# A two-layer transformer kernel with hand-written engine orders: another order of its start and its end, and the token permutation moved from VectorE to GpSimd and ScalarE

## The chip, the cores and the metric

One core of a Trainium2 chip, one launch. The metric is the device time of that core in microseconds (us). Five engines run their own instruction streams and wait for each other by semaphores: TensorE (matmuls and transposes), VectorE, ScalarE (activations and copies), GpSimd, and SyncE, whose queue here issues nearly all DMAs.

## The reference

The input `x` is 2 x 1024 tokens of 256 channels; everything is f32 unless said.

```
x  = L0_attn_x                                   # (2, 1024, 256)
xn = layernorm(x)
x  = x + L0_attn(xn) + L0_ffn(xn)
xn = layernorm(x)
x  = x + L1_attn(xn) + L1_ffn(xn)

L0_attn: q = rope(xn@Wq+bq) 32 heads of 8; k, v 8 heads of 8 (each serves 4 q heads)
         causal softmax(q k^T / sqrt 8) v over the 1024 tokens, @ Wo + bo
L0_ffn:  e4m3 inputs, bf16 results: (gelu(xn@Wg0) * (xn@Wg1)) @ Wl, hidden 1024
L1_attn: q, k, v 16 heads of 16, rope on q and k; the softmax runs over the 16 heads
         of one token: scores "bshd,bstd->bsht", then "bsht,bstd->bshd", @ wo^T
L1_ffn:  weights quantised to -s, 0, +s per group of 64; silu(gate)*up,
         RMS norm, @ w_proj^T, hidden 1024
```

Biases and some weights are scaled by constants before the call, which changes no shape.

## The kernel before, in words

The 2048 tokens are 16 tiles of 128, eight to a batch. Every step of every tile is a small Python function named by what it makes (`xnT.3` is step `xnT` of tile 3), and a table `ORDER` writes out for each engine in which order it runs its steps. Every step first waits on counting semaphores for its inputs and for its output buffer; an engine runs its steps strictly in the listed order, so a step that waits holds up all that are listed behind it. The same is true of SyncE's DMA issues. A second pass with exact number ranges stands behind a branch, and is not taken for these inputs; the steps `rng`, `rngb`, `fl` and `flagT` at the end decide that.

*Layer 0, attention.* For a tile: `ln0` (VectorE) and `rs0` (GpSimd) give mean and inverse deviation, `xn` the normalised tile, `xnT` its transpose (TensorE), `xnTc` the copy to SBUF, `qkv` the projection, `qkvc` the copy with bias, `va` the values, `wide` a range check. `rope` (four GpSimd instructions) turns q and k; `qh` (ScalarE) and `ql` (GpSimd) write the high and low half of q as f16, `q0` and `kl` (VectorE) those of k. `qt` and `kt` (SyncE) are DMA transposes of the two. Then come the *quads* Q: for tile n one for each earlier tile of its batch, itself, and each half of the heads: tile 0 has Q0 and Q1, tile 1 Q2 to Q5, tile 2 Q6 to Q11. `qk.Q` makes four score blocks of 128 x 512, `exp.Q` is two exponentials of 1024 columns, `mask.Q` (GpSimd, on the diagonal) zeroes the future, `pv.Q` is eight matmuls into the bank `psV`; `ob`, `obT`, `att`, `attT`, `attTc`, `wo0`, `xa` finish the tile.

*Layer 0, feed forward.* `up` (four a tile), on ScalarE `g`, `sq`, `fh`, `th` and on VectorE `ge1`, `ge3` for the gelu of each half, `down`, `yff`. The weights come by `wg` (SyncE) and `wgx` (ScalarE's queue) and are rounded to f8 by `w8.0` to `w8.5`. 

*Layer 1, attention.* `ln1`, `rs1`, `xn1`, `xs` (two f16 halves), `xt` (DMA transpose), `qkv1` (two a tile). The even part of `qkv1` holds q and k, the components on partitions and the 128 tokens in columns. `rab` (VectorE) multiplies it from PSUM by a cosine and a sine table, two instructions of 512 columns; `rr` (GpSimd) makes the difference and the sum, two of 256 columns; `rw` writes both to DRAM (`rscr`), `rd` reads them back so that four groups of 32 tokens lie in four partition quadrants (into `qk1T`), and `kq` (ScalarE, two copies of 512) puts them in the order in which `S1` (16 small f32 matmuls) wants them: for each of four j, 128 columns of 16 heads x 8 tokens. The tokens of one such group are 16 apart, since `vw` and `vr` bring the values in that order. So between PSUM and `S1` the tokens have to be permuted once; before, `rab` writes them transposed (token a*16+c to column c*8+a) and `kq` reads runs of eight. `ex1` (the exponentials), `PV1`, `o1r`, `o1T`, `o1`, `osum` (a range check), `ow` and `at1r` (through DRAM), `at1T`, `at1Tc`, `wo1`, `yo`.

*Layer 1, feed forward.* The three-valued weights are made once from `wt` loads by `tc`, `ts`, `tsc`, `tm`, `tcs`, `td`, `tde`, `tr`, `tw`. Then `gu` (four a tile), `tg`, `sg`, `hh`, `ssq`, `ssm`, `rsg`, `hxa`, `hx`, `ht` (DMA transpose), `dn1` (16 matmuls), `yout`, `out`.

*Loads and tables.* `first.0` x of tile 0, `first.1` Wqkv, `first.2` x of tiles 1 to 3; `lx` (ScalarE's queue) the rest of x; `lc` five small loads with Wo; `lw` the layer 1 attention weights (waits for `w8.3`), which `wh` and `wl` split; `wg.4` and `wg.5` wait for `w8.0` and `w8.1`, `wt.2` for `tc.0`. `tab` (VectorE, nine operations) reduces the angles of layer 1, `sin` (ScalarE) makes four tables of them and needs another activation table than the exponential. `tT`, `tTc` turn them.

*Warm products.* `warm.n` is `WARM[n]` matmuls of a block of ones into `psV` that nobody reads; before there are seven, 39 matmuls, all ahead of the first `pv`. The eight PSUM banks are four `psS`, `psV`, and `psA`, `psB`, `psC` that all other steps share in the order of `ORDER["pe"]`, each waiting for the reader of the bank's last content.

The order of TensorE's last steps before is, word for word:

```
        "qkv1.30 PV1.13 gu.57 qkv1.31 S1.14 o1T.13 gu.58 at1T.12 dn1.12 wo1.12 PV1.14 gu.59 gu.60 o1T.14 at1T.13 dn1.13 "
        "wo1.13 S1.15 gu.61 gu.62 PV1.15 gu.63 o1T.15 at1T.14 wo1.14 dn1.14 at1T.15 wo1.15 dn1.15 flagT.0"),
```

## Time and profile before

| what | value |
|---|---|
| median of 3 runs | 557.74 us (557.38 to 558.65) |
| the profiled execution | 560.62 us, its span 558.9 us |
| busy in the span: TensorE, ScalarE, VectorE, GpSimd | 520.7, 471.9, 381.5, 233.8 us |
| mean granted TensorE clock | 0.979 of full |
| DMA | 46.18 MB in 211344 packets |

The span is from the first to the last instruction of the profiled execution; its own time also has what lies around the span. An engine's busy time tells how much of the span it works, not whether anything waits for it; where two engines are full at once, the stretches, the waits and the chain of work that ended last have to be read together. A line number names a line of the kernel; a line in a helper serves many steps (L674 and L675 are every pair of transposes).

### The profile page before, as it was taken

The numbers are of one execution on the slowest core, as the hardware profiler recorded it, in microseconds if no ns is written. First come the engines' busy times: TensorE is split into PE (matmuls) and PEld (weight loads), VectorE is DVE, ScalarE is ACT, GpSimd is POOL, SyncE is SP. The second block draws the span as 40 slices with busy tenths as digits, with TensorE's granted clock in tenths as the row PEclk, the third lists the DMA queues.
The fourth block names the chain that finished last, engine by engine and source line by source line (L and its number), as shares of the span: only waits on it lengthen the run. The fifth ranks groups of instructions, "written<-read, shape, count | busy, mean of one in ns | idle before, by whom it ended". The sixth has DMA issues, their size and how long they took to land.

```text
span 558.9 us, 12847 instructions
## 1 busy us (share of the span) xinstructions
PE 520.7 (93%) x4872; PEld 261.7 (47%) x4920; DVE 381.5 (68%) x794; ACT 471.9 (84%) x614; POOL 233.8 (42%) x299
## 2 busy tenths in 40 slices
PE   7678999999999999999999999999999999998875
PEld 3323335434354555545555455564455353556544
DVE  5838887788779767766676787656554544756755
ACT  0579999999999999999989989988898998974440
POOL 3556745726534246344664565133082220160200
PEclk8869999999999999999999999999999999999988
DMA  7932112112443622345306454564533318347863
GB/s 246 326 84 58 26 41 57 41 33 39 76 82 47 103 47 59 53 66 79 67 12 122 62 83 67 93 99 67 110 56 66 64 40 142 67 83 130 112 112 88
DMA packets 211344, 46.18 MB, mean 83 GB/s; under 512 B 198544, under 2 KB 207888, under 8 KB 211280
## 3 DMA queue, kind: packets, MB, share of 16 engines
q1 hardware_dynamic: 208832, 42.37, 41.0%
q10 hardware_dynamic: 2448, 2.95, 1.7%
q8 instruction: 40, 0.66, 0.5%
q14 instruction: 24, 0.20, 0.1%
HBM read 19.09 MB, written 10.49 MB: 53 GB/s over the span
## 4 chain that ended last, share of the span: by engine, by line
PE 68%; ACT 13%; DVE 7%; DMA 5%; issue 4%; SPq 1%; POOL 1%; ACTq 0%; DVEq 0%
PE psV L775 20%; PE psS L761 8%; ACT Pt L1057 6%; PE psC L961 3%; PE psS L914 3%; PE psA L961 2%; PE psC L971 2%; PE psB L961 2%; DMA at<-o2scr 2%; DVE r L1512 2%; DMA stage<-in_wg 2%; PE psC L853 2%; PE psB L971 2%; PE psB L812 1%; PE psA L853 1%
## 5 line engine op out<-in xcount | busy, mean ns | idle before, releaser
L1057 ACT ACTIVATE Pt<-psS 128x1024 f32<-128x1024 f32 x288 | 279.9, 1031 | 27.2 <-PE psS L761 22.6
L775 PE MATMUL psV<-Pt,vaug 128*32 128x512 f32 x1152 | 150.6, 606 | 1.3 <-POOL Pt L1753 0.9
L1753 POOL TENSOR_SCALAR_AFFINE_SELECT Pt<-Pt 128x1024 f32<-128x1024 f32 x64 | 71.9, 1148 | 70.9 <-ACT Pt L1057 70.9
L761 PE MATMUL psS<-qTf,kTf 32*128 32x512 f16 x576 | 69.0, 388 | 7.7 <-DMA kTf<-QXf 4.2
L761 PEld LDWEIGHTS psS<-qTf,kTf 32*128 32x128 f16 x576 | 18.6, 91 | 92.3 <-ACT Pt L1057 47.0
L1805 POOL TENSOR_TENSOR ss<-ss,mhalf 128x1 f32<-128x1 f32 x16 | 9.3, 582 | 92.5 <-DVE ss L1589 92.5
L775 PEld LDWEIGHTS psV<-Pt,vaug 128*32 128x32 f32 x1152 | 25.0, 108 | 39.9 <-issue 31.1
L1131 ACT ACTIVATE stage<-psS 128x1024 f32<-128x1024 f32 x32 | 31.0, 1021 | 8.9 <-PE psS L914 8.8
L1799 POOL TENSOR_TENSOR rqkv<-r 128x256 f32<-128x256 f32 x32 | 24.9, 800 | 30.0 <-DVE r L1512 30.0
L1733 POOL TENSOR_TENSOR rt<-qkv,cs 128x320 f32<-128x320 f32 x16 | 15.1, 942 | 44.5 <-DVE QXf L1334 35.1
L1744 POOL TENSOR_TENSOR QXf<-rt,QXf 128x512 f16<-128x512 f32 x16 | 21.2, 1327 | 28.9 <-ACT QXf L1044 28.9
L1427 DVE SCALAR_TENSOR_TENSOR ga<-gw,gb 128x512 bf16<-128x512 f32 x32 | 23.1, 722 | 6.1 <-ACT gw L1083 6.1
L1418 DVE SCALAR_TENSOR_TENSOR gw<-gw,gb 128x512 f32<-128x512 f32 x32 | 25.1, 783 | 2.3 <-ACT gw L1072 2.2
L961 PE MATMUL psC<-wguT,xhs 128*128 128x512 bf16 x90 | 23.7, 380 | 2.4 <-issue 1.7
L1595 DVE SCALAR_TENSOR_TENSOR qtmp<-qtmp,ss 128x1024 f16<-128x1024 f32 x16 | 22.5, 1408 | 3.2 <-ACT qtmp L1152 3.2
L1152 ACT ACTIVATE qtmp<-qtmp,ss 128x1024 f16<-128x1024 f32 x16 | 18.5, 1158 | 4.5 <-POOL ss L1805 4.4
L1736 POOL TENSOR_TENSOR rt<-qkv,sn 128x160 f32<-128x160 f32 x32 | 21.9, 706 | 0.0
L1072 ACT ACTIVATE gw<-gb 128x512 f32<-128x512 bf16 x32 | 20.9, 653 | 0.0
L1083 ACT ACTIVATE gw<-gw 128x512 f32<-128x512 f32 x32 | 20.7, 646 | 0.0
L1512 DVE TENSOR_TENSOR r<-psC,big 128x512 f32<-128x512 f32 x14 | 14.5, 1120 | 8.9 <-PE psC L853 8.9
L1147 ACT ACTIVATE qtmp<-qtmp 128x1024 bf16<-128x1024 f32 x16 | 17.0, 1060 | 3.9 <-DVE qtmp L1583 2.4
L914 PE MATMUL psS<-kTf 24*128 24x128 f32 x512 | 19.5, 283 | 0.0
(339 smaller groups left out, 1088.1 us busy)
## 6 DMA issues: line engine op xcount, KB each, us to landing
rscr<-rqkv SPq DMA_DIRECT2D x32, 128.0 KB, 2.8
qk1T<-rscr SPq DMA_DIRECT2D x64, 64.0 KB, 3.0
vscr<-rqkv SPq DMA_DIRECT2D x16, 128.0 KB, 3.3
o2scr<-o SPq DMA_DIRECT2D x16, 128.0 KB, 1.7
at<-o2scr SPq DMA_DIRECT2D x16, 128.0 KB, 3.3
out<-yout SPq DMA_DIRECT2D x16, 128.0 KB, 2.7
x<-in_x ACTq DMA_DIRECT2D x3, 512.0 KB, 5.5
stage<-in_wg SPq DMA_DIRECT2D x2, 512.0 KB, 9.8
```

The lines of the kernel that those rows point to most:

```text
L761: e.matmul(psS[j], kd[32 * j:32 * j + k, h, 128 * at:128 * at + 128], qd[32 * j:32 * j + k, 4 * h:4 * h + 4, :].rearrange("p s n -> p (s n ...
L775: ins = e.matmul(psV[32 * j:32 * j + 32, :], vaug[:, at, j, 32 * h:32 * h + 32], Pt[(4 * Q + j) % NP], start=(kb == 0 and h == 0), stop=(k ...
L914: ins = e.matmul(psS[b][:, 128 * j:128 * j + 128], of_group(n, 1, b, j), of_group(n, 0, b, j), start=True, stop=True)
L961: ins = e.matmul(bank[:], src[:, pt, 128 * c:128 * c + 128], wguT[:, c, c0:c0 + 512], start=(k == 0), stop=(k == 3))
L1057: e.activation(flat(Pt4[:, u % NP:u % NP + 2, :]), flat(psS4[:, j:j + 2, :]), ACT.Exp, scale=scale).then_inc(S["exp"], 1)
L1131: e.activation(P1[:, 4 * b:4 * b + 8, :].rearrange("p g n -> p (g n)"), flat(psS4[:, b:b + 2, :]), ACT.Exp, scale=SC1).then_inc(S["ex1"], 1)
L1418: e.scalar_tensor_tensor(gw[:, half, :], gw[:, half, :], 1.0 / GA, gb[:, half, :], ALU.add, ALU.mult).then_inc(S["ge1"], 1)
L1427: e.scalar_tensor_tensor(a, gw[:, half, :], 1.0, gg, ALU.add, ALU.mult).then_inc(S["ge3"], 1)
L1512: e.tensor_tensor(r1[:, k, :].rearrange("p (e s c a) -> p e s a c", e=2, s=2, a=8), bank, table.unsqueeze(2).to_broadcast([128, 2, 2, 8, 1 ...
L1595: e.scalar_tensor_tensor(hx_b[:, 1, :], h1, sn[:, 2:3], hx_b[:, 0, :], ALU.mult, ALU.subtract).then_inc(S["hx"], 1)
L1753: e.affine_select(out=p, in_=p, pattern=[[0, 8], [1, 128]], compare_op=ALU.is_ge, fill=0.0, base=0, channel_multiplier=-1).then_inc(S["mas ...
L1799: e.tensor_tensor(dst[:, 256 * f:256 * f + 256], r1[:, f, 0:256], r1[:, f, 256:512], op).then_inc(S["rr"], 1)
```

## The change

Five things change at once.

1. SyncE's and ScalarE's queues at the start: `lc`, then `wt.0`, `wg.0`, `wg.1`, then the transposes `qt.0 kt.0`, and only then the loads that wait (`wg.4`, `lw.0`, `wg.5`, `wt.1`, `wt.2`). On ScalarE `lx.1 lx.2` go first, `wgx` after `tc.0`, `sin.0` before `exp.0`, and `g`, `fh`, `sq` of the first halves and `wh.0` behind the first exponentials. On VectorE `qkvc.0`, `tab.0`, `q0.0 kl.0` go ahead of the weight roundings `w8`; on TensorE `up.0` to `up.3` go behind the first quads.
2. The permutation: `rab` writes its products in plain token order; `rr` reads runs of four tokens 16 apart and writes contiguously; the scratch `rscr` is laid out with the quadrant ahead of q and k; `kq` reads with a step of four floats (16 bytes) from SBUF; the constant `same` of the second pass follows.
3. `WARM` is now 24 matmuls in four places at the start and 14 in six places (`warm.4` to `warm.9`) among the last steps; those wait for the last `ob`, when `psV` is free.
4. The range check `rng.0` moves behind `at1Tc.15`; in the drain `rd.15` goes ahead of `out.11`, `dn1.13` ahead of `at1T.13`, `osum.14` behind other steps.
5. All five orders are written anew; most steps move by a few places.

The set of steps is the same but for the warm products. The diff, cut to its core:

```
 KQ = 2
-WARM = (9, 3, 2, 7, 5, 11, 2)
+COLD = 4
+WARM = (9, 3, 10, 2, 3, 2, 2, 3, 2, 2)
...
-        "warm.0 xnT.0 qkv.0 warm.1 xnT.1 warm.2 qkv.1 warm.3 up.0 up.1 up.2 ts.0 warm.4 ts.1 up.3 warm.5 qk.0 warm.6 "
...
+        "warm.0 xnT.0 qkv.0 warm.1 xnT.1 qkv.1 warm.2 xnT.2 ts.0 qkv.2 qk.0 warm.3 qk.1 ts.1 pv.0 qk.2 pv.1 up.0 qk.3 "
+        "up.1 xnT.3 up.2 obT.0 pv.2 qk.4 td.0 td.1 up.3 pv.3 qk.5 up.4 up.5 qkv.3 pv.4 qk.6 up.6 up.7 qk.7 pv.5 xnT.4 "
...
+        "S1.14 o1T.13 gu.58 at1T.12 dn1.12 wo1.12 PV1.14 gu.59 gu.60 warm.4 o1T.14 warm.5 dn1.13 at1T.13 warm.6 wo1.13 "
+        "S1.15 gu.61 gu.62 PV1.15 gu.63 o1T.15 at1T.14 dn1.14 wo1.14 warm.7 at1T.15 warm.8 wo1.15 warm.9 dn1.15 flagT.0"),
...
-        "wgx.2 wgx.3 qh.0 g.0 tc.0 g.1 sq.0 fh.0 fh.1 wh.0 qh.1 sq.1 lx.1 lx.2 exp.0 th.0 exp.1 sin.0 exp.2 exp.3 qh.2 "
+        "lx.1 lx.2 qh.0 tc.0 wgx.2 wgx.3 sin.0 qh.1 exp.0 exp.1 exp.2 lx.3 g.0 exp.3 fh.0 sq.0 g.1 qh.2 sq.1 th.0 wh.0 "
+        "tde.0 exp.4 tde.1 fh.1 exp.5 fh.2 th.1 g.2 exp.6 sq.2 fh.3 g.3 exp.7 th.2 exp.8 exp.9 g.4 qh.3 sq.3 exp.10 "
...
-        "vz.0 ln0.0 xn.0 idc.0 xnTc.0 ln0.1 ln0.2 xn.1 qkvc.0 w8.0 xnTc.1 va.0 w8.1 w8.2 wide.0 w8.3 q0.0 qkvc.1 ln0.3 "
+        "vz.0 ln0.0 xn.0 idc.0 xnTc.0 ln0.1 ln0.2 qkvc.0 xn.1 wide.0 va.0 xnTc.1 tab.0 q0.0 kl.0 qkvc.1 xn.2 xnTc.2 "
+        "wide.1 va.1 ln0.3 w8.0 w8.1 q0.1 kl.1 qkvc.2 ln0.4 tsc.0 wide.2 tsc.1 w8.2 w8.3 xn.3 ob.0 xnTc.3 tm.0 va.2 "
...
+        "hh.28 v1c.15 o1.13 at1Tc.12 sg.29 yo.12 yout.12 hh.29 osum.13 o1r.14 sg.30 ssm.14 o1.14 osum.14 at1Tc.13 hx.14 "
+        "yo.13 yout.13 hh.30 sg.31 o1r.15 hh.31 o1.15 at1Tc.14 ssm.15 osum.15 hx.15 yo.14 at1Tc.15 yout.14 rng.0 rngb.0 "
+        "yo.15 yout.15 fl.0"),
...
-        "first.0 first.1 first.2 wg.0 wg.1 wg.4 wt.0 lc.0 wt.1 lw.0 wg.5 wt.2 qt.0 kt.0 qt.1 kt.1 qt.2 kt.2 qt.3 wt.3 "
+        "first.0 first.1 first.2 lc.0 wt.0 wg.0 wg.1 qt.0 kt.0 wg.4 qt.1 kt.1 lw.0 wg.5 wt.1 wt.2 qt.2 kt.2 qt.3 wt.3 "
+        "kt.3 qt.4 wt.4 wt.5 qt.5 xt.0 kt.4 xt.1 rw.0 mk.0 kt.5 rw.1 rd.0 xt.2 vw.0 rd.1 vr.0 ht.0 qt.6 xt.3 vw.1 kt.6 "
...
-        "vw.13 rd.12 vr.12 ow.11 vw.14 vr.13 at1r.11 rd.13 rw.14 ht.12 xt.15 rd.14 ow.12 vr.14 at1r.12 rw.15 ow.13 "
-        "vw.15 ht.13 at1r.13 out.11 rd.15 out.12 vr.15 ow.14 ht.14 at1r.14 ow.15 at1r.15 out.13 ht.15 out.14 out.15"),
+        "ht.13 at1r.13 rd.15 out.11 out.12 ow.14 vr.15 ht.14 at1r.14 ow.15 out.13 at1r.15 ht.15 out.14 out.15"),
...
-        rscr = nc.dram_tensor("rscr", [NT, 2, 4, 16, 512], F32, kind="Internal").ap()
+        rscr = nc.dram_tensor("rscr", [NT, 4, 2, 16, 512], F32, kind="Internal").ap()
         vscr = nc.dram_tensor("vscr", [NT, 16, 128, 16], F32, kind="Internal").ap()
         o2scr = nc.dram_tensor("o2scr", [NT, 16, 128, 16], F32, kind="Internal").ap()
         oscr = nc.dram_tensor("oscr", [NT, 128, 256], F32, kind="Internal").ap()
...
             return (qk1Tg if n < NT else qk1T)[:, s, :, :]
 
         def landed(s):
-            return qk1T[:, s, :, :].rearrange("p j n -> p (j n)").rearrange("p (h j a) -> p j h a", j=4, a=8)
+            return qk1T[:, s, :, :].rearrange("p j n -> p (j n)").rearrange("p (m j) -> p j m", j=4)
+
+        def by_run(a):
+            return a.rearrange("p (m b j) -> p b m j", b=4, j=4)
 
         def of_group(n, s, b, j):
 
...
 
             def rw(n):
                 src = flat(rqkv[n % 2][:, 0:2, :]).rearrange("p (f m t) -> p f m t", f=2, t=32)
-                dst = rscr[n].rearrange("s b (f i) (h t) -> f (i h) (s b) t", f=2, t=32)
+                dst = rscr[n].rearrange("b s (f i) (h t) -> f (i h) (b s) t", f=2, t=32)
                 for f in range(2):
                     w.wait_ge("rr", 2 * n + f + 1)
                     e.dma_start(dst[f], src[:, f, :, :]).then_inc(S[f"d_rw{n % 2}"], 16)
...
                 w.wait_ge("kq", KQ * n)
                 for b in range(4):
                     dst = qk1T[32 * b:32 * b + 16, :, :, :].rearrange("p s j n -> p s (j n)")
-                    e.dma_start(dst, rscr[n, :, b].rearrange("s d n -> d s n")).then_inc(S[f"d_rd{n % 2}"], 16)
+                    e.dma_start(dst, rscr[n, b].rearrange("s d n -> d s n")).then_inc(S[f"d_rd{n % 2}"], 16)
 
             def ow(n):
                 w.wait_ge("o1", 2 * n + 2)
...
 
             def warm(n):
                 w.wait_ge("zero", 5)
+                w.wait_ge("ob", NT if n >= COLD else 0)
                 for _ in range(WARM[n]):
                     e.matmul(psV[:], blockb[:], blockb[:].unsqueeze(1).to_broadcast([128, 4, 128]), start=True, stop=True)
 
...
                 w.wait_ge(f"d_rd{n % 2}", read_groups(n))
                 w.wait_ge("S1", 4 * n)
                 for s in range(2):
-                    e.activation(qk1Tg[:, s, :, :].rearrange("p j (h a) -> p j h a", a=8), landed(s), ACT.Copy).then_inc(S["kq"], 1)
+                    e.activation(qk1Tg[:, s, :, :], landed(s), ACT.Copy).then_inc(S["kq"], 1)
 
             def ex1(n):
                 w.wait_ge("w8", 6)
...
                                 ALU.mult).then_inc(S["v1c"], 1)
 
             def rab(n):
-                bank = psM[filled["qkv1", 2 * n] % len(psM)][:].rearrange("p (e s a c) -> p e s a c", e=2, s=2, a=8)
+                bank = psM[filled["qkv1", 2 * n] % len(psM)][:].rearrange("p (e s t) -> p e s t", e=2, s=2)
                 t0 = 128 * (n % NB)
                 w.wait_ge("tTc", 5)
                 w.wait_ge("tc", 12)
                 w.wait_ge("qkv1", 2 * n + 1)
                 w.wait_ge("rr", 2 * n)
                 for k in range(2):
-                    table = turns[:, k:k + 2, t0:t0 + 128].rearrange("p e (a c) -> p e a c", a=8)
-                    e.tensor_tensor(r1[:, k, :].rearrange("p (e s c a) -> p e s a c", e=2, s=2, a=8), bank,
-                                    table.unsqueeze(2).to_broadcast([128, 2, 2, 8, 16]), ALU.mult).then_inc(S["rab"], 1)
+                    e.tensor_tensor(r1[:, k, :].rearrange("p (e s t) -> p e s t", e=2, s=2), bank,
+                                    turns[:, k:k + 2, t0:t0 + 128].unsqueeze(2).to_broadcast([128, 2, 2, 128]),
+                                    ALU.mult).then_inc(S["rab"], 1)
 
             def ro1(n):
                 cb = cos1[:, n % NB, :].unsqueeze(1).unsqueeze(1).to_broadcast([128, 2, 16, 8])
...
                 w.wait_ge("rab", 2 * n + 2)
                 w.wait_ge(f"d_rw{n % 2}", 32 * (n // 2))
                 for f, op in enumerate((ALU.subtract, ALU.add)):
-                    e.tensor_tensor(dst[:, 256 * f:256 * f + 256], r1[:, f, 0:256], r1[:, f, 256:512], op).then_inc(S["rr"], 1)
+                    e.tensor_tensor(dst[:, 256 * f:256 * f + 256].rearrange("p (b m j) -> p b m j", b=4, j=4),
+                                    by_run(r1[:, f, 0:256]), by_run(r1[:, f, 256:512]), op).then_inc(S["rr"], 1)
 
             def rsg(n):
                 sn = ss[n % len(ss)]
...
     s[:, :, 0::2] *= -1
     mneg = np.where(p[None, :] > p[:, None], np.float32(NEG), np.float32(0))
     pos = (np.arange(8)[None, :] * 128 + p[:, None]).astype(np.float32)
-    same = (np.arange(512)[None, :] % 8 == np.arange(8)[:, None]).astype(np.float32)
+    same = (np.arange(512)[None, :] // 4 % 8 == np.arange(8)[:, None]).astype(np.float32)
     ind2 = np.stack([NEG * same, 1.0 - same]).astype(np.float32)
     one = (p[:, None] // 16 == np.arange(8)[None, :]).astype(np.float32)
     ind1 = np.stack([NEG * one, 1.0 - one], axis=1).astype(np.float32)
```

## Rows read from the trace of the kernel before

**Rows 1.** Stretches: us, each engine's busy time (instructions), granted clock, DMA share, GB/s.

```profile
60.00:250.00 190.00, 182.71 (x1680) 88.62 (x1692) 147.34 (x302) 186.01 (x252) 89.99 (x111) 1.00 0.31 56
250.00:495.00 245.00, 242.08 (x2370) 120.78 (x2388) 154.53 (x324) 221.90 (x280) 101.27 (x128) 1.00 0.44 75
530.00:559.00 29.00, 18.15 (x148) 12.51 (x147) 14.96 (x41) 8.48 (x12) 1.10 (x2) 0.88 0.54 105
```

The busy times are those of PE, PEld, DVE, ACT and POOL, in that order.

**Rows 2.** The chain that ended last, before 60 us: start, duration, what.

```profile
21.35 2.01 SPq L608
23.46 6.31 DMA kTf<-QXf
```

**Rows 3.** ScalarE's instructions in order of time, 30 to 60 us: start, duration.

```profile
30.49 1.94 ACT L1057 ACTIVATE Pt<-psS 128x1024 f32<-128x1024 f32 x2 [3.93 <-PE psS L761]
...
34.79 1.28 ACT L1018 ACT_TABLE_LOAD   x1
...
39.13 1.28 ACT L1057 ACT_TABLE_LOAD   x1 [0.56 <-PE psV L775]
...
48.81 3.96 ACT L1057 ACTIVATE Pt<-psS 128x1024 f32<-128x1024 f32 x4
```

**Rows 4.** GpSimd's instructions in order of time, tile 0's rope and `ql`.

```profile
11.67 1.17 POOL L1733 TENSOR_TENSOR rt<-qkv,cs 128x320 f32<-128x320 f32 x1 [0.19 <-DVE qkv L1303]
...
15.96 1.15 POOL L1744 TENSOR_TENSOR QXf<-rt,QXf 128x512 f16<-128x512 f32 x1 [0.74 <-ACT QXf L1044]
```

**Rows 5.** Stretch 19 to 24 us, busy time of `tab` alone (VectorE, then ScalarE).

```profile
19.00:24.00 5.00, 3.92 (x9) 0.00 (x0) 0.70 1.05 394
```

**Rows 6.** Line 600, the key transposes: from issue to landing.

```profile
DMA to landing us min/median/max: 2.3/2.8/6.3
```

**Rows 7.** Groups of instructions by line: busy us, mean ns, idle before, releasers.

```profile
L1512 DVE TENSOR_TENSOR r<-psC,big 128x512 f32<-128x512 f32 x14 | 14.5, 1120 | 8.9 <-PE psC L853 8.9
L1583 DVE SCALAR_TENSOR_TENSOR qtmp<-stmp,psB 128x512 f32<-128x512 f32 x13 | 8.9, 686 | 5.6 <-PE psB L961 5.3
L1799 POOL TENSOR_TENSOR rqkv<-r 128x256 f32<-128x256 f32 x32 | 24.9, 800 | 30.0 <-DVE r L1512 30.0
L1744 POOL TENSOR_TENSOR QXf<-rt,QXf 128x512 f16<-128x512 f32 x16 | 21.2, 1327 | 28.9 <-ACT QXf L1044 28.9
L1122 ACT ACTIVATE kTf<-qk1T 128x512 f32<-128x512 f32 x32 | 18.6, 642 | 0.1
```

**Rows 8.** Line 1512, `rab`: who waited for it, us and times.

```profile
  PEld psA L858: 1.2, 1
```

**Rows 9.** TensorE's instructions in order of time, from 530 us.

```profile
533.07 0.33 PE L674 MATMUL psB<-identf,at 128*128 128x128 f32 x1 [2.96 <-DMA at<-o2scr]
...
533.35 2.98 PE L971 MATMUL psC<-wpT,stmp 128*128 128x256 bf16 x16
...
537.73 1.17 PE L914 MATMUL psS<-kTf 24*128 24x128 f32 x32
...
546.51 1.91 PE L971 MATMUL psC<-wpT,stmp 128*128 128x256 bf16 x16
...
553.34 2.48 PE L971 MATMUL psC<-wpT,stmp 128*128 128x256 bf16 x16
```

**Rows 10.** Other engines' instructions in order of time, from 530 us.

```profile
531.88 1.06 ACT L1147 ACTIVATE qtmp<-qtmp 128x1024 bf16<-128x1024 f32 x1 [1.57 <-DMA stmp<-qtmp]
...
535.12 1.15 ACT L1122 ACTIVATE kTf<-qk1T 128x512 f32<-128x512 f32 x2
...
548.50 1.32 SPq L624 DMA_TRANSPOSE stmp<-qtmp  x1
548.53 0.68 DVE L1625 TENSOR_REDUCE hl<-rec 128x1 f32<-128x512 f32 x1
...
551.00 0.41 DVE L1602 COPY at1T<-psA 128x256 f32<-128x256 f32 x1
```

**Rows 11.** DMA issues by line: count, and median us from issue to landing.

```profile
stmp<-qtmp SPq DMA_TRANSPOSE x16, 4.2
```

29 lines of the change are left out of this document (17 added, 12 removed), and 232 rows, old and new, of the table ORDER.

## The prediction

> **What bounds the kernel now.** I read the stretches first. From 60 to 250 us ScalarE is busy 186.01 of 190 us and TensorE 182.71; from 250 to 495 us TensorE is busy 242.08 of 245 us and ScalarE 221.90; from 530 us on nobody is full (TensorE 18.15 of 29 us) and the granted clock falls to 0.88 [rows 1]. So there are four stages: a start in which the softmax cannot begin, a stage set by ScalarE, one set by TensorE with ScalarE 10% free, and a drain of dependent steps. VectorE and GpSimd bound none of them; an edit of theirs counts only by whom it lets go earlier.
>
> The chain that ended last tells what holds the start: not arithmetic, but SyncE's queue reaching the first transposes at 21.35 and 23.46 us, and 6.31 us until the keys landed [rows 2]. ScalarE's order of time shows the first exponentials at 30.49 us, Q6's (the end of tile 1, start of tile 2) in the row that starts at 48.81 us, and two table loads of 1.28 us around `sin` in between [rows 3].
>
> **Part A, the start.** Tile 0's rope begins at 11.67 us, 0.19 us after GpSimd was free of the three `rs0`, which precede it in both orders; so it does not move. `ql.0` ends at 15.96 + 1.15 = 17.11 us [rows 4]. `qt.0` could go then, but SyncE still stood at `lw.0`, `wg.5` and `wt.2`, which wait for `w8` and `tc.0`. The new order puts `qt.0 kt.0` ahead of every bulk load that waits. `lc` comes first now because `tab.0` precedes `q0.0 kl.0` on VectorE; the nine `tab` operations take 3.92 us and some gaps, say 4.2 us [rows 5]. From the end of `xnTc.1`, some 1 us after tile 0's rope began, that gives `kl.0` at 17.6 us if `lc`'s five loads have landed, as bulk loads now stand behind and not before them. `qt.0` takes 2.01 us of queue as before, so `kt.0` is issued at 19.2 us instead of 23.46: 4.3 us earlier.
>
> The landing is unknown, as other loads share the 16 engines: `lx.1`, `lx.2` now go early, the two `wgx` loads (1 MB) at about 17.7 us. Bounds are the fastest key transpose, 2.3 us, and the 6.3 us of this one [rows 2, 6]; with less outstanding than before I take 4.3, the middle. Then keys are there at 23.5 us. Four score matmuls (0.6 us) and a table load follow: `sin.0` now runs before `exp.0`, which therefore has to load its table again, and a load stands behind the wait of its instruction, as the row at 39.13 us shows. So `exp.0` starts at 23.5 + 0.6 + 1.28 = 25.4 us, not 30.49.
> [...]
>
> From `exp.0` to the start of Q6 the kernel before took 20.2 us (half of the 3.96 us row is Q5, so Q6 is at 50.7 us). I listed ScalarE's steps before Q6 in both orders: they are the same set. So the shift there is what ScalarE idles less. `sin` with its loads (34.79 to 40.42 us, 5.6 us) leaves this stretch; `g` `fh` `sq` of halves 0 and 1 (six steps of some 0.5 us, start to start) and `wh.0` (1.5 us), 4.5 us in all, enter it, as `up.0` to `up.3` and `lw.0` now come later. A new hole stands between `exp.1` and `exp.2`: `qk.2` is behind `pv.0`, which waits for GpSimd's mask (two of 1.1 us), some 1.8 us. Q6 is at 25.4 + 20.2 - 5.6 + 4.5 + 1.8 = 46.3 us, 4.4 us earlier. The next tile's chain (`rope.2` after `mask.1` at 30.4 us, `qh.2`, `ql.2`, transposes) gives keys by 44 us, before they are needed. With the landing's bounds it is 2.4 to 6.4 us.
>
> Does it last? As long as ScalarE is the bound, yes, since the set of its steps is the same; but TensorE has only 7.3 us free from 60 to 250 us and 2.9 after [rows 1]. Its moved work (four `up` later, one `xnT` and `qkv` earlier) about cancels. I take 3.5 of 4.4 us; ends 0 (all lost to TensorE) and 6.
>
> **Part B, the permutation.** `rab` writes with a step of eight floats and takes 1.12 us; `hh`, also 512 f32 elements with one operand in PSUM, but contiguous, takes 0.69 us [rows 7]. Contiguous `rab` should be 0.69: 32 x 0.43 = 13.8 us less of VectorE, which is hidden except where somebody waits. TensorE waited for `rab` to free a bank a few times, 1.2 us at most [rows 8]. Four to five such waits can each shrink by up to 2 x 0.43 = 0.86 us, but some only pass to the next step. I take 1.2 us, ends 0 and 4.
>
> `rr` on GpSimd (800 ns, 256 elements) now reads runs of four floats. `ql`, 512 elements with a broadcast, takes 1327 ns [rows 7]: its price follows the count and not the pattern. I keep 0.80 us, at the dearest 1.33; GpSimd has idle time all along but for the drain, where two would cost 1 us. The DMA sides of `rw` and `rd` keep their pieces (128 bytes and 2 KB), so nothing is taken for them.
>
> `kq` is the doubtful one. It read runs of eight floats; now every element is 16 bytes from the last. It takes 642 ns for 512 elements [rows 7], no more than fits the exponential's 0.97 us for 1024 [rows 3], so its runs of eight cost nothing today and a gain is excluded; no row has ScalarE reading with a step. The lower bound is no change. The upper bound is what the step costs VectorE in `rab`, 0.43 us each. I take no change, since `rab`'s step is twice as wide and on the write side, and keep both ends.
> The Trainium skill (Advanced Engine Details and Errata, "SBUF Cachelines") says that two accesses should fall into one 16-byte line, and that a new line at each access is penalised. By that rule `kq` pays; `rab`'s row agrees for a step of 32 bytes, no row here tests 16. It speaks against this change and is the first rival below.
>
> **Part C, the drain.** Three things move. First, `rd.15` stood behind `out.11` in SyncE's queue and `dn1.13` behind `at1T.13`, for which TensorE idled 2.96 us until 533.07; then `dn1.13` ran slowly (2.98 us against 1.91 for the 16 matmuls of `dn1.14`) [rows 9], and `S1.15` came only at 537.73. Now `dn1.13` runs when its transpose has landed (`ssq.14` waited for the same until 531.88) [rows 10], in that hole, with warm products around it, and `wo1.13` ends at 535.6. `S1.15` then waits for `kq.15`, which ends at 535.12 + 1.15 = 536.3 [rows 10] behind `hxa.14` and does not move: 1.4 us gained. Second, `osum.14` leaves the place before `hh.31`: 0.3 us. Third, the range checks `rng` (from 548.53 us) stood before `at1Tc.15` (551.00) and now come after, so `wo1.15` starts about 1.5 us earlier. `dn1.15` then waits for its transpose `ht.15`, issued at 548.50 before [rows 10] and at 546.8 now; with the median of such a landing, 4.2 us [rows 11], it starts at 551.0 and takes 1.9 us, where it ran from 553.34 for 2.48 [rows 9]. The end of TensorE's work moves from 555.8 to 552.9: 2.9 us in all, of which 1.7 are the first two. `rng` and `rngb` still fit beside `dn1.15`. The 14 warm products cost at most 14 x 0.22 = 3 us where they delay; they stand in front of waits, so I take 0. Upstream, `rab.14` and `rab.15` are on the chain: 0.6 us more. Part C: 3.5 us, ends 1 (what the transposes' landings give is lost) and 5.
>
> **The sum.** 3.5 + 1.2 + 3.5 = 8.2 us. The profiled execution took 560.62 us, its span 558.9; it becomes 552.4. The median of the runs shown is 557.74, 2.9 below that execution: 549.5 us.
>
> **The rivals.**
> - ScalarE pays for `kq` (20%). 32 x 0.43 = 13.8 us. Eight of them before 250 us count fully, 3.4 us; sixteen between 250 and 495 us, 6.9 us against 23.1 us of ScalarE's idle time, one third, 2.3; in the drain two on the way to `S1.15`, 0.9. Together 6.6: 556.1 us. For it: `rab`'s price for a step. Against it: half the step, another engine.
> - The slower side (10%): the same price, but none is hidden, because `kq` stands ahead of exponentials for which TensorE waits: 549.5 + 13.8 = 563.3. It decides from 8.2 / 32 = 0.26 us per `kq` on. For it: ScalarE 98% busy until 250 us [rows 1]. Against it: its 10% free later.
> - The start is given back (18%). TensorE is 96% busy until 250 us and 99% after, with the same work; if its order cannot be packed tighter, only B and C are left, 553.0 us. Against it: it has 7.3 us free in the stage in which ScalarE leads.
> - More than forecast (8%): keys land at 2.3 us and all of it lasts, `rab`'s waits all go: 6 + 3 + 4 = 13 us, 544.7.
> - It does not do what it says (6%): the early `lc`, `wt.0` and `lx` hold up `wqkv` or `kt.0`, whose landing takes over 9 us, and the drain's landings set its end: within 0.2% of 557.7.
>
> **How the numbers follow.** My forecast has 38%, its own range 546.5 to 552. 0.2%, 1.1 us, is what a measurement can tell from no change. Faster are forecast, first, third and fourth: 38 + 20 + 18 + 8 = 84%; same 6%, slower 10%. From 544.5 to 557.5 us leaves out the slower rival, part of the fourth and part of the fifth case, not quite 20%.
>
> **What would show it.** `kt.0` issued near 19 us, the first exponential near 25, Q6 near 46; `rab` at 0.69 and `rr` at 0.80 us; `kq` at 0.64 (1.07 makes the first two rivals live); the 60 to 250 us stretches unchanged in kind; no 3 us hole before `at1T.13`, and a granted clock above 0.88 at the end. I am wrong if the transposes' landings stretch or if ScalarE's reading step costs.

## The result, and the profile after

The changed kernel takes 565.83 us (median of 4 runs, 564.83 to 567.54) where the kernel before takes 557.98 in the same comparison (4 runs, 557.38 to 558.65): ratio 1.0148, 95% interval 1.0113 to 1.0182. It is 7.9 us slower; the forecast was 549.5 us, 8.2 faster. The profiled execution of the changed kernel took 564.83 us, its span 563.1.

First the groups of instructions by line, of the changed kernel; they answer to [rows 7].

```profile
L1516 DVE TENSOR_TENSOR r<-psC,big 128x512 f32<-128x512 f32 x12 | 7.7, 685 | 7.2 <-PE psC L858 7.2
L1588 DVE SCALAR_TENSOR_TENSOR qtmp<-stmp,psB 128x512 f32<-128x512 f32 x14 | 9.6, 685 | 8.9 <-PE psB L966 8.6
L1804 POOL TENSOR_TENSOR rqkv<-r 128x256 f32<-128x256 f32 x32 | 26.7, 856 | 19.0 <-DVE r L1516 19.0
L1749 POOL TENSOR_TENSOR QXf<-rt,QXf 128x512 f16<-128x512 f32 x16 | 20.1, 1256 | 36.0 <-ACT QXf L1049 36.0
L1127 ACT ACTIVATE kTf<-qk1T 128x512 f32<-128x512 f32 x32 | 35.0, 1157 | 2.0 <-DMA qk1T<-rscr 2.0
```

`rab` fell from 1120 to 685 ns, to the price of `hh` as forecast; `rr` went from 800 to 856. But `kq`, forecast at 642, takes 1157 ns: 0.515 us more, 32 times, 16.5 us of ScalarE. And that now has waiters; this is the view of waits (us in total, times, the longest). PEld is TensorE's load of the weights, PE the matmul behind it: both lines show the same four stalls, so they are not added. All four lie behind 495 us, in the drain:

```profile
PEld psS L919 <- ACT kTf L1127: 6.2, 4, 2.1
PE psS L919 <- ACT kTf L1127: 4.8, 4, 1.7
```

The stretches of the changed kernel, as [rows 1]:

```profile
60.00:250.00 190.00, 184.11 (x1710) 88.27 (x1708) 148.67 (x302) 187.78 (x249) 92.23 (x118) 1.00 0.31 59
250.00:495.00 245.00, 240.97 (x2320) 119.42 (x2316) 146.81 (x315) 224.57 (x272) 94.68 (x117) 1.00 0.40 71
530.00:563.00 33.00, 24.94 (x205) 15.15 (x201) 16.96 (x45) 9.86 (x12) 1.10 (x2) 0.90 0.62 101
```

They look as before: ScalarE is 99% busy until 250 us and 92% after, TensorE 97 and 98%. The busy shares don't tell that one kernel is slower; the only hint is a count, 272 instructions of ScalarE between 250 and 495 us where the kernel before has 280. Where a busy share is already near full, added work shows as a longer span and not as a fuller stretch.

The start went a little better than forecast. The chain that ended last, before 60 us, answers to [rows 2]:

```profile
16.13 1.36 SPq L612
17.60 5.22 DMA kTf<-QXf
```

`kt.0` is issued at 17.60 us and not at 23.46 (19.2 forecast), and the keys take 5.22 us to land, between my bounds of 2.3 and 6.3. ScalarE's order of time answers to [rows 3]:

```profile
21.53 1.28 ACT L1062 ACT_TABLE_LOAD   x1
23.32 3.77 ACT L1062 ACTIVATE Pt<-psS 128x1024 f32<-128x1024 f32 x4 [0.50 <-PE psS L766]
29.25 1.02 ACT L1062 ACTIVATE Pt<-psS 128x1024 f32<-128x1024 f32 x1 [2.16 <-PE psS L766]
...
45.43 1.95 ACT L1062 ACTIVATE Pt<-psS 128x1024 f32<-128x1024 f32 x2
```

The first exponential starts at 23.32 us (30.49 before, 25.4 forecast): the table load, at 21.53 us, lies beside the landing of the keys and not behind it. The hole for `pv.0` is there, 2.16 us. Q6 starts at 45.4 instead of 50.8 us: 5.4 earlier, where I forecast 4.4.

The drain, TensorE's order of time, answers to [rows 9]:

```profile
534.76 1.92 PE L976 MATMUL psB<-wpT,stmp 128*128 128x256 bf16 x16
...
540.46 1.88 PE L919 MATMUL psS<-kTf 24*128 24x128 f32 x32 [1.75 <-ACT kTf L1127]
...
554.21 0.34 PE L678 MATMUL psA<-identf,at 128*128 128x128 f32 x1 [2.86 <-DMA at<-o2scr]
...
554.56 1.06 PE L707 MATMUL psV<-blockb 128*128 128x512 bf16 x2
...
558.11 1.91 PE L976 MATMUL psC<-wpT,stmp 128*128 128x256 bf16 x16
```

`dn1.13` sits in the old hole and takes 1.92 us (2.98 before). But TensorE waits 1.75 us for `kq.15`, and 2.86 us before `at1T.15`, where it waited 0.67 before:

```profile
549.09 0.33 PE L674 MATMUL psA<-identf,at 128*128 128x128 f32 x1 [0.67 <-DMA at<-o2scr]
```

**When each part of the loss falls.** The start of the n-th of the 288 exponentials (two per quad), in us, read from ScalarE's order of time. c_kqplain is the changed kernel with `kq` reading as it lies, h_front and a_oldperm have the old permutation (all below).

```
n                   0     12     60    132    160    200    240    287
before           30.5   50.8  130.3  251.8  298.1  366.4  429.2  494.1
changed          23.3   45.4  124.8  248.5  294.6  365.7  430.2  496.5
c_kqplain        22.8   45.0  124.4  245.2  290.3  358.7  421.6  486.2
a_oldperm        24.7   46.4  125.8  248.1  293.2  362.1  425.1  490.3
h_front          23.1   44.7  125.1  246.5  292.8  361.1  423.9  488.8
kq steps done       0      0      0      4      5      8     10     12
```

At the 60th the changed kernel still leads by 5.5 us; the first `kq` runs at 147 us; from there the lead goes, and at the last exponential it is 2.4 us behind.

### The profile page after: what moved, and what is told of

Same layout as the page of the kernel before. It is cut to its first block, busy times and chain, and to the rows that moved or that the text cites. A ratio compares the mean times of both kernels' runs of the same rounds, so it can differ in the third digit from the quotient of the medians.

```text
span 563.1 us, 12894 instructions
## 1 busy us (share of the span) xinstructions
PE 529.0 (94%) x4919; PEld 263.0 (47%) x4919; DVE 377.3 (67%) x794; ACT 487.5 (87%) x614; POOL 232.0 (41%) x299
## 4 chain that ended last, share of the span: by engine, by line
PE 63%; ACT 19%; issue 7%; DMA 4%; DVE 2%; POOL 2%; SPq 2%; ACTq 0%; POOLq 0%; DVEq 0%
PE psV L780 19%; ACT Pt L1062 11%; PE psS L766 8%; ACT kTf L1127 4%; PE psS L919 3%; PE psB L966 3%; PE psA L966 2%; PE psC L966 2%; PE psC L976 2%; PE psC L817 1%; PE psA L858 1%; PE psB L817 1%; DMA x<-in_x 1%; PE psB L831 1%; DMA qk1T<-rscr 1%
## 5 line engine op out<-in xcount | busy, mean ns | idle before, releaser
L1758 POOL TENSOR_SCALAR_AFFINE_SELECT Pt<-Pt 128x1024 f32<-128x1024 f32 x64 | 70.6, 1129 | 78.3 <-ACT Pt L1062 78.3
L766 PE MATMUL psS<-qTf,kTf 32*128 32x512 f16 x576 | 69.5, 387 | 8.5 <-ACT Pt L1062 7.1
L766 PEld LDWEIGHTS psS<-qTf,kTf 32*128 32x128 f16 x576 | 18.7, 91 | 90.5 <-ACT Pt L1062 51.6
L1127 ACT ACTIVATE kTf<-qk1T 128x512 f32<-128x512 f32 x32 | 35.0, 1157 | 2.0 <-DMA qk1T<-rscr 2.0
L1804 POOL TENSOR_TENSOR rqkv<-r 128x256 f32<-128x256 f32 x32 | 26.7, 856 | 19.0 <-DVE r L1516 19.0
L1423 DVE SCALAR_TENSOR_TENSOR gw<-gw,gb 128x512 f32<-128x512 f32 x32 | 26.5, 830 | 5.8 <-ACT gw L1077 5.8
L919 PE MATMUL psS<-kTf 24*128 24x128 f32 x512 | 22.6, 293 | 6.8 <-ACT kTf L1127 4.8
L1432 DVE SCALAR_TENSOR_TENSOR ga<-gw,gb 128x512 bf16<-128x512 f32 x32 | 25.6, 799 | 1.2 <-ACT gw L1088 1.1
L966 PE MATMUL psB<-wguT,xhs 128*128 128x512 bf16 x92 | 24.6, 391 | 0.0
L919 PEld LDWEIGHTS psS<-kTf 24*128 24x128 f32 x512 | 18.5, 192 | 12.3 <-ACT kTf L1127 6.2
L966 PE MATMUL psA<-wguT,xhs 128*128 128x512 bf16 x84 | 21.7, 380 | 0.0
L1077 ACT ACTIVATE gw<-gb 128x512 f32<-128x512 bf16 x32 | 20.9, 654 | 0.1
```

The source lines that it names most:

```text
L766: e.matmul(psS[j], kd[32 * j:32 * j + k, h, 128 * at:128 * at + 128], qd[32 * j:32 * j + k, 4 * h:4 * h + 4, :].rearrange("p s n -> p (s n ...
L919: ins = e.matmul(psS[b][:, 128 * j:128 * j + 128], of_group(n, 1, b, j), of_group(n, 0, b, j), start=True, stop=True)
L966: ins = e.matmul(bank[:], src[:, pt, 128 * c:128 * c + 128], wguT[:, c, c0:c0 + 512], start=(k == 0), stop=(k == 3))
L1127: e.activation(qk1Tg[:, s, :, :], landed(s), ACT.Copy).then_inc(S["kq"], 1)
L1423: e.scalar_tensor_tensor(gw[:, half, :], gw[:, half, :], 1.0 / GA, gb[:, half, :], ALU.add, ALU.mult).then_inc(S["ge1"], 1)
L1432: e.scalar_tensor_tensor(a, gw[:, half, :], 1.0, gg, ALU.add, ALU.mult).then_inc(S["ge3"], 1)
```

## The experiments

Each was compared with the kernel before on the same chip, which took 557.6 to 558.2 us there. Kernels whose difference turned out to change nothing (d_rrall and r_out13_d below) lie up to 2.2 us apart, so a single difference smaller than that shows nothing by itself.

**1. What the new permutation and the new orders are worth.** a_oldperm is the changed kernel with the permutation of before, b_newperm the kernel before with the new permutation alone.

```diff
-                    e.tensor_tensor(r1[:, k, :].rearrange("p (e s t) -> p e s t", e=2, s=2), bank,
+                    e.tensor_tensor(r1[:, k, :].rearrange("p (e s c a) -> p e s a c", e=2, s=2, a=8), bank,
...
-                    e.activation(qk1Tg[:, s, :, :], landed(s), ACT.Copy).then_inc(S["kq"], 1)
+                    e.activation(qk1Tg[:, s, :, :].rearrange("p j (h a) -> p j h a", a=8), landed(s), ACT.Copy).then_inc(S["kq"], 1)
```

This is a_oldperm against the changed kernel, cut to two of its places; b_newperm is the same the other way round in the kernel before.

> The changed kernel with the token permutation of before (rab writes with a step of eight floats, rr plain, kq reads runs of eight), all new orders and warm products kept. Theory 1 (ScalarE pays for kq's step of four floats: 1157 ns instead of 642, 32 x 0.515 = 16.5 us of ScalarE, is the whole loss): the 5.4 us won before Q6 last and the drain gives some more, 549 to 553 us; kq back at 0.64 us, rab at 1.11. Theory 2 (the new orders lose what the start won, kq is hidden): within 2 us of the changed kernel, 563 to 567 us.

> The kernel before with the new permutation alone, orders and warm products of before. Theory 1: 16.5 us more of ScalarE, of which the part up to 250 us and that in the drain count and some of the middle, less about 1 us for the faster rab: 565 to 571 us. Theory 2: 556 to 559 us.

Measured: a_oldperm 555.13 us, ratio 0.9948 (0.9918 to 0.9977); b_newperm 569.33, ratio 1.0187 (1.0131 to 1.0243). So the permutation loses 11.5 us on the old orders (569.33 less 557.87) and 10.7 on the new ones (565.83 less 555.13), and the orders with the unread products gain 2.7 us, less than the 4.4 us that a_oldperm had won by Q6.

**2. `kq` alone, and the same permutation without it.** c_kqplain lets `kq` copy in the order that lies in memory; it leaves out the last part of the permutation, so its layer 1 mixes the wrong tokens and only its time counts. d_rrall gives the whole transposition to GpSimd's sums and leaves the layout in memory and `kq` as before.

```diff
-            return qk1T[:, s, :, :].rearrange("p j n -> p (j n)").rearrange("p (m j) -> p j m", j=4)
+            return qk1T[:, s, :, :].rearrange("p j n -> p (j n)").rearrange("p (j m) -> p j m", j=4)
```

```diff
-                    e.tensor_tensor(dst[:, 256 * f:256 * f + 256].rearrange("p (b m j) -> p b m j", b=4, j=4),
-                                    by_run(r1[:, f, 0:256]), by_run(r1[:, f, 256:512]), op).then_inc(S["rr"], 1)
+                    e.tensor_tensor(dst[:, 256 * f:256 * f + 256].rearrange("p (s c a) -> p s c a", s=2, a=8),
+                                    r1[:, f, 0:256].rearrange("p (s a c) -> p s c a", s=2, a=8),
+                                    r1[:, f, 256:512].rearrange("p (s a c) -> p s c a", s=2, a=8), op).then_inc(S["rr"], 1)
```

> The changed kernel in which kq copies its 512 columns in the order in which they lie (the permutation of the last two token bits is left out, so layer 1's attention mixes other tokens); every other instruction is as in the changed kernel. Theory 1: kq at 0.62 to 0.65 us and the time of a_oldperm less the faster rab, 548 to 552 us. Theory 2: 563 to 567 us.

> The changed kernel's orders, rab contiguous, and the whole transposition in GpSimd's rr, which reads with a step of 16 floats and writes contiguously; scratch layout and kq (runs of eight) as before. Theory 1: kq 0.64, rab 0.68; if rr takes 0.9 to 1.3 us it stays hidden but in the drain: 549 to 553 us. If GpSimd pays for a step as ScalarE does (1.6 us and more) it adds some 2 us to the drain: 551 to 555. Theory 2: 563 to 567 us.

Measured: c_kqplain 552.75 us, ratio 0.9873 (0.9813 to 0.9934); d_rrall 551.05, ratio 0.9865 (0.9811 to 0.9919). The lines of `kq` in c_kqplain, and of `rr` and `kq` in d_rrall:

```profile
L1127 ACT ACTIVATE kTf<-qk1T 128x512 f32<-128x512 f32 x32 | 18.6, 640 | 2.8 <-DMA qk1T<-rscr 2.8
```

```profile
L1801 POOL TENSOR_TENSOR rqkv<-r 128x256 f32<-128x256 f32 x32 | 38.4, 1223 | 17.6 <-DVE r L1513 17.6
...
L1124 ACT ACTIVATE kTf<-qk1T 128x512 f32<-128x512 f32 x32 | 18.6, 640 | 2.0 <-DMA qk1T<-rscr 2.0
```

One line of code, 640 instead of 1157 ns, is worth 565.83 - 552.75 = 13.1 of the 16.5 us that it saves on ScalarE. The table above shows how evenly: the changed kernel falls behind c_kqplain by 3.3, 4.3, 7.0, 8.6 and 10.3 us when 4, 5, 8, 10 and 12 `kq` steps have added 4.1, 5.2, 8.3, 10.3 and 12.4 us. Of that distance 0.4 us was there before the first `kq`; without it 70 to 80% has landed at each mark, and from the 132nd to the last exponential, the stretch in which ScalarE has 8 to 10% idle, 7.0 us of 8.3. So the loss lands before 250 us and after it alike.

How it gets there shows in TensorE's waits between 60 and 495 us. First the changed kernel, then c_kqplain:

```profile
PE psS L766 <- ACT Pt L1062: 4.6, 11, 0.5
PE psS L919 <- ACT Pt L1062: 1.8, 6, 0.3
```

```profile
PE psS L766 <- ACT Pt L1062: 1.4, 5, 0.5
```

In this stretch nobody is seen waiting for `kq` itself. TensorE's score matmuls (L766 `qk`, L919 `S1`) wait for the exponentials, which read the banks `psS` and stand behind `kq` in ScalarE's order: 6.4 us against 1.4. That is 5.0 of the 9.9 us that the changed kernel loses there; waits too short for this view are not in it.

In d_rrall GpSimd's sums are 0.42 us longer each than in the kernel before (800 ns), 13.5 us in all (10.7 against a_oldperm, whose sums take 890), and none of it can be seen in the time.

**3. Where the rest of the start's lead goes.** f_rrall_b is the kernel before with the plain `rab` of the changed kernel and the `rr` of d_rrall. h_front has the old permutation, the new orders up to about 130 us and the orders of before from there on; i_rest is its other half. g_nowarm is a_oldperm without the last fourteen unread products. The edit of h_front against a_oldperm, shown for ScalarE behind `exp.30`:

```diff
-exp.31 sq.9 exp.32 qh.6 sq.10 th.9 tde.10 exp.33 tde.11
+exp.31 sq.9 exp.32 qh.6 sq.10 exp.33 th.9 tde.10 tde.11
...
```

and that of g_nowarm:

```diff
-WARM = (9, 3, 10, 2, 3, 2, 2, 3, 2, 2)
+WARM = (9, 3, 10, 2, 0, 0, 0, 0, 0, 0)
```

> The orders and the unread products of the kernel before, with one change: VectorE's products rab lie plainly, and GpSimd's sums rr do the whole transposition, reading with a step of 16 floats; kq and the layout in memory stay as before. It parts the gain of the best run so far (551.05 us, of which the new orders alone, in a_oldperm, gave 2.7) into orders and rearrangement. If the 0.43 us saved on each of the 32 rab counts where products of the second layer wait for VectorE, and the 13.5 us added to GpSimd lie beside other work: 558 less 4 (551.05 against 555.13), 553 to 555 us, with rab at 685 ns and rr at 1223. Rival: the rearrangement pays only with the new orders, since before's order puts VectorE at rest after rab: 557 to 558 us. Second rival: GpSimd's longer sums come late for the rotations in an order not made for them: 559 us or more.

> Old permutation everywhere; the changed kernel's orders up to the second quad of tile 15's predecessors, about 130 us (TensorE's first 151 steps, ScalarE's first 106, VectorE's 128, GpSimd's 37, SyncE's 39, and the unread products 9, 3, 10, 2 of the start), then the orders of before; no unread products at the end. At 130 us the new start led by 5.4 us in the changed kernel and by 4.5 in a_oldperm, which ended only 2.7 us early. If the lead is lost to the new orders of the later stretches, this kernel keeps it: 553 to 554 us. Rival: the lead is lost in any order, since a later tile is paced by VectorE and TensorE and not by when the first exponential ran: 555 to 556 us, as a_oldperm. The exponentials' starts show where the lead shrinks.

> The other half: old permutation, the orders of before up to about 130 us with their unread products, and the changed kernel's orders from there on, with its unread products at the end. If the new orders of the later stretches cost what the lead lost, 558 to 560 us; if the loss is in neither half alone, 558 as before; if the new drain helps by the 3.5 us that I forecast for it and the middle costs nothing, 554 to 555 us.

> a_oldperm without the fourteen unread products of the last 30 us (the numbers from 3, 2, 2, 3, 2, 2 to none). If they keep the granted clock up and so shorten dn1 and wo1 of the last tiles, as my third term had it, this is 1 us or more slower than a_oldperm's 555.13 us; if they only fill waits and the clock sits where it sat, the same within 0.5; if they delay the products behind them, up to 1 us faster. The last dn1 (1.91 us in the changed kernel, 2.48 in the one before) and the granted clock from 495 us on decide.

Measured: f_rrall_b 555.95 us, ratio 0.9964 (0.9943 to 0.9985); h_front 553.62, 0.9920 (0.9891 to 0.9949); i_rest 561.74, 1.0069 (1.0047 to 1.0090); g_nowarm 553.36, 0.9922 (0.9894 to 0.9950).

The new start alone is worth 4.2 us, with the orders of before behind it: in its profile the lead is 6.1 us at Q6 and still 5.3 at the last exponential, so most of what is won in the first 45 us reaches the end. The plain `rab`, each time with another reading in `rr`, comes out at 1.9 us on the old orders (557.86 to 555.95) and at 2.4 on the new ones (a_oldperm to c_kqplain); both are at the edge of what a single comparison can tell. Two later pairs give 0.5 (h_front to k_front_rrall) and 0.7 (g_nowarm to j_rrall_nowarm), a_oldperm to d_rrall 4.1. The new orders behind 130 us are worth nothing: with the new start they end at 555.13 or, without the unread products, 553.36, beside h_front's 553.62. On the old start they lose 3.9.

**4. The unread products at the end, and the versions in which gains are joined.** m_after_nowarm, l_rest_nowarm and j_rrall_nowarm are the changed kernel, i_rest and d_rrall, each with the edit of g_nowarm; k_front_rrall is h_front with the plain `rab` and the edit of d_rrall.

> The changed kernel whole, without the fourteen unread products of its last 30 us. With the old permutation these products cost 1.8 us (555.13 with them, 553.36 without): in the profile of a_oldperm two groups of 1.06 us stand between at1T.15, wo1.15 and dn1.15 at the lower clock, with no wait between them. If that is what they do, the changed kernel falls from 565.8 to 563.5 or 564.5 us. Rival: the difference of g_nowarm came by chance from an earlier landing of at1r.15 (idle 2.42 us instead of 4.05 us): then no change, 565 to 566.5.

> i_rest (start of before, new orders from 130 us on, old permutation, 561.74 us) without the fourteen unread products at the end. If these products are the whole loss of i_rest against before, 558 us; if the new later orders lose by themselves what the last exponential shows (1.2 us later than before), 559 us; if the products cost the 1.8 us seen so far and the orders the rest, 560 us.

> d_rrall (551.05 us: the changed kernel's orders, plain rab, the whole transposition in rr) without the unread products at the end. If they cost 1.8 us here as well: 549 to 549.5 us, the fastest version so far. If not: 551.

> h_front (new start to 130 us, then the orders of before, 553.62 us) with plain rab and the whole transposition in rr, which gave 1.9 us on the orders of before and 4.1 on the new ones. If the gains add: 551.7 by the first number, 549.5 by the second. If the new later orders are no better than the old ones once the unread products are out, this and j_rrall_nowarm end within 1 us of each other.

Measured: m_after_nowarm 565.85 us, ratio 1.0129 (1.0081 to 1.0177); l_rest_nowarm 560.88, 1.0048 (1.0022 to 1.0074); j_rrall_nowarm 552.65, 0.9902 (0.9863 to 0.9940); k_front_rrall 553.12, 0.9896 (0.9859 to 0.9933). Without the fourteen products the time changes by 0.0, -0.9, +1.6 and (g_nowarm) -1.8 us: no effect that can be told, and my reading of g_nowarm, that they cost 1.8 us, fell. The profiles show why there may be none: without these products `dn1.15` takes 2.99 to 3.45 us in all four, with them 1.91 to 2.78 in the eleven kernels that have them, but two groups of them stand before it (1.06 us each at the lower clock in a_oldperm and c_kqplain). k_front_rrall ends within 0.5 us of j_rrall_nowarm, but it gained only 0.5 us on h_front, not the 1.9 or more expected. Why the gains don't add there was not pursued; by the other pairs above, the gain of the plain `rab` itself is uncertain.

**5. What sets `kq`'s price.** All but the last change only `kq`'s two access patterns in the changed kernel: n_step2 reads every second float, o_step8 every eighth, p_kqwrite reads plainly and writes with a step of four; all three leave the tokens in another order than the masks assume, and only their times count. e_rrwrite is d_rrall with the step of `rr` on its write.

```diff
-            return qk1T[:, s, :, :].rearrange("p j n -> p (j n)").rearrange("p (m j) -> p j m", j=4)
+            return qk1T[:, s, :, :].rearrange("p j n -> p (j n)").rearrange("p (h m j) -> p h j m", h=2, j=2)
...
-                    e.activation(qk1Tg[:, s, :, :], landed(s), ACT.Copy).then_inc(S["kq"], 1)
+                    e.activation(qk1Tg[:, s, :, :].rearrange("p (h j) n -> p h j n", h=2), landed(s), ACT.Copy).then_inc(S["kq"], 1)
```

That is n_step2; o_step8 does the same with `"p (m j) -> p j m", j=8` and `"p j (x m) -> p (j x) m"`. Then p_kqwrite and e_rrwrite (against d_rrall):

```diff
-                    e.activation(qk1Tg[:, s, :, :], landed(s), ACT.Copy).then_inc(S["kq"], 1)
+                    e.activation(qk1Tg[:, s, :, :].rearrange("p j n -> p (j n)").rearrange("p (m j) -> p j m", j=4), landed(s), ACT.Copy).then_inc(S["kq"], 1)
```

```diff
-                    e.tensor_tensor(dst[:, 256 * f:256 * f + 256].rearrange("p (s c a) -> p s c a", s=2, a=8),
-                                    r1[:, f, 0:256].rearrange("p (s a c) -> p s c a", s=2, a=8),
+                    e.tensor_tensor(dst[:, 256 * f:256 * f + 256].rearrange("p (s c a) -> p s a c", s=2, a=8),
+                                    r1[:, f, 0:256].rearrange("p (s a c) -> p s a c", s=2, a=8),
...
```

> The changed kernel with kq reading every second float (8 bytes) in place of every fourth; so two token bits in the queries and keys of layer 1 lie otherwise than the masks assume. If the price grows with the step in bytes: kq halfway, some 0.81 to 0.90 us, and 556 to 560 us in whole (c_kqplain 552.75, the changed kernel 565.8). If any step costs the full price: 1.16 us and 565 to 566 us. If only a step of 16 bytes or more costs: 0.64 us and 552 to 554 us.

> The same with kq reading every eighth float (32 bytes), in eight runs of 64. If the price grows with the step: above 1.16 us, up to 2.2 us if it doubles, and over 575 us. If it is the same for 16 bytes and more: 1.16 us and 565 to 566 us.

> The changed kernel with kq reading plainly and writing with a step of four floats (order of the tokens in layer 1 other than the masks assume). If ScalarE pays for a step of 16 bytes on either side: 1.16 us each and 565 to 566 us. If it pays only for reading: 0.64 us and 552 to 554 us, as c_kqplain.

> d_rrall with the transposition of rr on the side of the write: both sources read plainly, the result written with a step of 8 floats. d_rrall's rr, which reads both sources with a step of 16 floats, took 1223 ns against 800 plain. If GpSimd pays for each source read in steps, rr is near 800 to 900 ns here; if for a write too, 1200 ns. Either way the time stays at 551 to 553 us if GpSimd's sums lie beside other work, as d_rrall's 13.5 us of longer sums did; under 550 us if they do not.

The lines of `kq` in n_step2, o_step8 and p_kqwrite, and of `rr` in e_rrwrite:

```profile
L1127 ACT ACTIVATE kTf<-qk1T 128x512 f32<-128x512 f32 x32 | 20.2, 694 | 2.0 <-DMA qk1T<-rscr 2.0
```

```profile
L1127 ACT ACTIVATE kTf<-qk1T 128x512 f32<-128x512 f32 x32 | 35.0, 1155 | 2.4 <-DMA qk1T<-rscr 2.4
```

```profile
L1127 ACT ACTIVATE kTf<-qk1T 128x512 f32<-128x512 f32 x32 | 33.7, 1174 | 1.9 <-DMA qk1T<-rscr 1.9
```

```profile
L1801 POOL TENSOR_TENSOR rqkv<-r 128x256 f32<-128x256 f32 x32 | 27.1, 869 | 17.8 <-DVE r L1513 17.8
```

Times: 553.23 us, ratio 0.9921 (0.9897 to 0.9944); 568.23, 1.0151 (1.0087 to 1.0215); 563.25, 1.0104 (1.0071 to 1.0137); e_rrwrite 552.62, 0.9887 (0.9855 to 0.9919). The price is a threshold and no slope: 694 ns at 8 bytes, 1157 at 16, 1155 at 32, and a write with a step of 16 costs the same 1174. Cheap `kq`: 553 us. Dear `kq`, whichever the reason: 563 to 568. o_step8 lies 2.4 us above the changed kernel and p_kqwrite 2.6 below it with nearly the same mean price; in p_kqwrite the two copies of a step overlap more (33.7 us busy against 35.0), the rest of the 5 us is not explained.

**6. One more moved step.** The new orders put `out.13` between `ow.15` and `at1r.15` on SyncE's queue. q_out13_a (a_oldperm) and r_out13_d (d_rrall) put it back.

```diff
-        "ht.13 at1r.13 rd.15 out.11 out.12 ow.14 vr.15 ht.14 at1r.14 ow.15 out.13 at1r.15 ht.15 out.14 out.15"),
+        "ht.13 at1r.13 rd.15 out.11 out.12 ow.14 vr.15 ht.14 at1r.14 ow.15 at1r.15 out.13 ht.15 out.14 out.15"),
```

> a_oldperm (555.13 us) with at1r.15 ahead of out.13 in SyncE's queue, as in the order of before. If out.13's transfer holds up the landing of ow.15, for which at1r.15 waits, at1r.15 is issued 1.7 us after ow.15 and not 2.6 or 3.9, TensorE waits under 1.5 us before at1T.15, and the time is 553.5 to 554.2. If the landings are slow for another reason, the wait stays at 1.8 to 4.6 us and the time at 555.

> d_rrall (551.05 us) with the same exchange. If out.13 is the cause: 549.5 to 550.3 us, the fastest version, with TensorE waiting under 1.5 us before at1T.15. If not: 551 to 552.

Measured: q_out13_a 555.43 us, ratio 0.9931 (0.9904 to 0.9957); r_out13_d 553.25, 0.9919 (0.9885 to 0.9952). No gain, and TensorE still waits, here in r_out13_d:

```profile
541.11 0.33 PE L675 MATMUL psA<-identf,at 128*128 128x128 f32 x1 [4.06 <-DMA at<-o2scr]
```

The theory fell. SyncE's order of time shows what is late: `at1r.15` (`at<-o2scr`) waits until `ow.15` (`o2scr<-o`) has landed. First h_front, with the old late order, then r_out13_d:

```profile
536.93 0.32 SPq L610 DMA_DIRECT2D o2scr<-o  x1
538.63 0.37 SPq L616 DMA_DIRECT2D at<-o2scr  x1
```

```profile
534.14 0.32 SPq L580 DMA_DIRECT2D o2scr<-o  x1
538.17 0.37 SPq L586 DMA_DIRECT2D at<-o2scr  x1
```

1.70 us in one, 4.03 in the other, for the same 128 KB.

What differs is in the DMA view of just this stretch. First h_front (536.93 to 538.62 us), then r_out13_d (534.14 to 538.15):

```profile
q1 hardware_dynamic: 144, 0.13, 22.6%
```

```profile
q1 hardware_dynamic: 144, 0.13, 10.1%
q8 instruction: 1, 0.02, 1.5%
```

The same 144 packets go out; in r_out13_d one packet of 16 KB on the instruction queue goes out beside them. The trace names that queue `instruction`; I take its packets, 40 in each profile, for loads of the program. I looked for them at `ow.15` in all 20 profiles. In the seven where none runs beside it (before, h_front, f_rrall_b, b_newperm, i_rest, g_nowarm, m_after_nowarm) it lands after 1.68 to 1.70 us. In eleven of the thirteen where one does, it lands after 2.5 to 4.0 us, always 2.1 to 2.8 us after that packet started; d_rrall and p_kqwrite, with 1.85 and 1.71 us, are spared, and why is not known. Over all tiles of all profiles, writes of `ow` with no other data beside them land after 1.68 to 1.72 us without such a packet (104 of them) and after 1.69 to 4.01 with one (22). So the late landing goes with a program load that falls on it, and at `ow.15` never comes without one. No run moved the load on purpose, and each kernel has one profile only. But taking out the fourteen products moved it in two kernels from 0.3 and 1.1 us after the issue (the changed kernel, a_oldperm) to 7.4 us after it (m_after_nowarm, g_nowarm), and there the landing took 1.70 us; in the other two pairs this is not so.

## Why the prediction was wrong, step by step

**The step that failed** is `kq` in part B: "I take no change, since `rab`'s step is twice as wide and on the write side". Neither reason held. A step twice as wide costs ScalarE the same (1155 against 1157 ns), and the write side is no different (1174). The upper bound failed too: 0.43 us was VectorE's price, ScalarE's is 0.515. ScalarE's threshold lies between 8 and 16 bytes, so "half the step" of `rab` was still on the dear side of it. The Trainium skill (Advanced Engine Details and Errata, "SBUF Cachelines") had it: by its rule, at least two accesses should fall into a 16-byte line. The runs agree on ScalarE, at both steps around that limit. I cited it as a rival and gave the rival too little weight against an argument that no row supported.

**How much of it lands** was the error of the first rival: I let a third of `kq`'s price count between 250 and 495 us because ScalarE has 10% idle there. Measured, 7.0 of 8.3 us lands between the 132nd and the last exponential, about as much as elsewhere. Idle time of an engine that runs in turns with the bound one was not free room here: `kq` stands ahead of exponentials in ScalarE's order, and TensorE, itself full, waits for these exponentials (6.4 us against 1.4 in c_kqplain). The waits for `kq` itself (weight loads: 3.0 us in c_kqplain, 6.2 in the changed kernel) come only in the drain. The waits seen cover half of the loss; that the rest goes the same way is argued, and no run tested it alone.

The second rival, nothing hidden, was nearest: its 563.3 us with 0.515 in place of 0.43 would be 566.0. That this meets 565.83 is luck: a fifth of the price was hidden (3.4 us), and the rest of the forecast gained 3.1 us less than the 8.2 that the rival took over.

**Part A** held, in part by luck. Q6 came 5.4 us earlier (forecast 4.4), and 4.2 us reach the end (h_front; forecast 3.5). But its terms missed both ways: `kt.0` was issued 1.6 us earlier than forecast, its landing took 0.9 longer, the table load, 1.28 us in the sum, cost nothing, since ScalarE loaded before the scores were there, and from the first exponential to Q6 it took 22.1 us and not 20.9. The rival that the start is given back is out.

**Part B, `rab`**: 685 ns as forecast; worth 0.5 to 4.1 us by five pairs of kernels, where I took 1.2. `rr`: 856 against 800 ns with four-float runs; but a_oldperm, whose `rr` is plain, has 890 with the new orders, and b_newperm, with four-float runs and the old orders, 814, so the new reading costs nothing that can be seen. That GpSimd's price follows the count alone is wrong, as d_rrall's 1223 ns at a step of 16 floats shows.

**Part C** was worth nothing instead of 3.5 us. In the four profiles with the old late orders and the cheap `kq` (before, h_front, k_front_rrall, f_rrall_b) and the eleven with the new ones I read the end in three legs, means in us:

```
                                  old late orders    new late orders
last exponential to S1.15         42.5 (41.4-43.6)   41.7 (41.2-42.4)
S1.15 to start of dn1.15          15.0 (14.7-15.6)   16.5 (14.3-18.0)
duration of dn1.15                2.06 (1.91-2.48)   2.65 (1.91-3.45)
last exponential to end of span   62.6 (61.1-64.8)   63.9 (62.1-65.9)
```

The first leg gains 0.8 us, half of what refilling `dn1.13`'s hole was to give (1.7 with `osum.14`). The second loses 1.5, where the earlier `at1Tc.15` was to gain 1.2: `ow.15` lands after 1.7 us in three of the four profiles (2.86 in the fourth), but after 1.7 to 4.0 us in the new ones, so that the chain waits for the transfer and not for the range checks. Experiment 6 shows what goes with it: a program load beside the transfer, in one of the four profiles and in nine of the eleven. The third loses 0.6, with a lower granted clock: from 530 us on it is 0.88 to 0.99 in the four and 0.83 to 0.92 in the eleven. The unread products shortened `dn1.15` but did not bring the old value back.

I also counted one thing twice. Part C was read off an execution whose drain was 64.8 us, the longest of the four, and I then took off the 2.9 us by which that execution stood above the median. Part of what was to be gained was in those 2.9 already: `dn1.15`, 2.48 us there, takes 1.91 or 1.92 in the three others in the same order, so the 0.6 us that I took for it were that execution's own. The slow `dn1.13`, 2.98 us, was not: it takes 3.33 and 3.28 in f_rrall_b and k_front_rrall, and 1.91 in h_front only.

**The sum as measured**: 557.9 - 2.7 (start, late orders, unread products: a_oldperm) - 2.4 (`rab`, to c_kqplain) + 13.1 (`kq`) = 565.9 us. It ends at the 565.83 by construction, as each term is the difference of two kernels on the way from one to the other; it tells the sizes and is no check of them.

Open is also why the new late orders lose 3 to 4 us behind the old start (i_rest, l_rest_nowarm) and nothing behind the new one. Their last exponential is only 0.3 to 1.2 us later than before's, so it would have to lie in the drain; but their profiled executions don't show it whole (spans of 557.4 and 560.3 us, before 558.9).

d_rrall, the fastest, needs none of the new layout in memory. 551.05 us is its own median; its relatives (j_rrall_nowarm, e_rrwrite, r_out13_d, k_front_rrall) lie between 552.6 and 553.3, so the honest figure for all of them is 551 to 553 us, 4.5 to 7 faster than the kernel before.

## What to carry to other kernels

- When a rearrangement is moved between engines, the price of its step must be known on the engine that gets it. Another engine's price is no bound for it: here VectorE's 0.43 us was taken and ScalarE's was 0.515, 1.8 times the plain copy. And such a step belongs on the engine with idle time on no chain (here GpSimd: 13.5 us more, nothing in the time), not on one that is 90 to 99% busy.
- Ten per cent of idle time on an engine that alternates with a full one hid about a fifth of the work added to it, not two thirds.
- Holes near the end of one execution can be that execution's own (`dn1.15`, 2.48 against 1.91 us) or the order's (`dn1.13`): where the execution stands above the median, don't take off the difference and count the hole too.
- A transfer that lands late for no reason in its own queue may share the DMA engines with a load of the program: ask the DMA view of that stretch for the instruction queue. Fourteen matmuls fewer moved it by some 7 us here.

## What the runs showed that I had not expected

- ScalarE copying 512 f32 elements per partition: 640 ns plain, 694 with an 8-byte step, 1157 at 16 bytes, 1155 at 32, 1174 when the 16-byte step is on the write. Runs of eight floats, 32 bytes each, cost nothing (642).
- VectorE's product of 512 f32 writes with a 32-byte step in 1120 ns and plainly in 685. GpSimd's sum of 256 f32 takes 800 to 890 ns plain (the higher values with the new orders), 869 with a 32-byte step on the write, 1223 when both sources are read with a 64-byte step.
- The same 128 KB write to memory takes 1.68 to 1.72 us to land when no other data and no 16 KB packet of the program runs beside it, and up to 4.0 us when one does.
- The table load before the first exponential cost nothing although it stood in its way in the order: ScalarE loaded at 21.53 us, before the scores were there.
